# Where a head's row sums are closed: Q in slot 0, the fold on GpSimd, a first block written by ScalarE

## The reference

```python
x = layernorm(x + self_attention(x))                       # 32 heads of 16, causal, rotary
# cross-attention with ctx (4 x 1601 x 512): 32 query heads of 128, 8 key/value heads
q = (x @ Wq + bq).reshape(B, L, 8, 4, 128)
k, v = split(ctx @ Wkv + bkv)                              # 8 heads of 128 each
s = einsum('blkgd,bmkd->bkglm', q, k) / sqrt(128)
o = einsum('bkglm,bmkd->blkgd', softmax(s), v)
x = layernorm(x + o.reshape(B, L, 4096) @ Wo + bo)
x = layernorm(x + x @ base_W.T + top2_gated_lora(x))       # 28 experts of rank 8
```

## Time and profile before

| what | before |
|---|---|
| median of 3 runs | 3050.05 us (3045.78 to 3051.54) |
| profiled execution | 3042.88 us, span 3041.1 us |
| PE busy | 2831.5 us (93%) |
| DVE / ACT / POOL busy | 2171.2 / 1906.0 / 1570.0 us |
| chain that ended last | PE 78%, issue 7%, ACT 6%, POOL 3%, DVE 3%, DMA 2% |
| granted TensorE clock, mean | 0.985 |

### The profile page before, as it was taken

The page is one execution under the profiler, slowest core; times in us unless marked ns, Lnnn a source line. Parts: engine busy times, 40 slices in busy tenths (PEclk is TensorE's granted clock), DMA queues, the critical chain, the costliest instruction groups (busy, mean ns, idle before and its releaser), DMA issues.

```text
span 3041.1 us, 60253 instructions
## 1 busy us (share of the span) xinstructions
PE 2831.5 (93%) x20784; PEld 2619.2 (86%) x20784; DVE 2171.2 (71%) x4492; ACT 1906.0 (63%) x4264; POOL 1570.0 (52%) x1535
## 2 busy tenths in 40 slices
PE   7899999998899999999889999999978999999996
PEld 6789999997689999999668999999967899999985
DVE  5587777777558777777665877777756587878785
ACT  4476666665557666666565766666646576666663
POOL 4288787755125555555511645454542254555553
PEclk9999999998999999999899999999989999999998
DMA  5356564513311112121321112121222121212112
GB/s 186 134 190 208 165 215 162 178 50 115 103 42 56 70 64 77 63 77 63 121 89 43 65 62 77 64 77 56 80 111 89 36 84 42 97 43 91 50 53 97
DMA packets 97915, 285.08 MB, mean 94 GB/s; under 512 B 9936, under 2 KB 18256, under 8 KB 94416
## 3 DMA queue, kind: packets, MB, share of 16 engines
q1 hardware_dynamic: 97616, 281.24, 27.1%
HBM read 237.16 MB, written 44.04 MB: 92 GB/s over the span
## 4 chain that ended last, share of the span: by engine, by line
PE 78%; issue 7%; ACT 6%; POOL 3%; DVE 3%; DMA 2%; DVEq 0%; SPq 0%; ACTq 0%; POOLq 0%
PE bank L1012 41%; PE dn L1012 18%; PE sp L1012 14%; PE sp L1143 2%; ACT ph L702 2%; POOL kept_s L524 1%; ACT orw L713 1%; PE sp L1232 1%; PE sp L1083 1%; PE sp L1151 1%; ACT pn L629 1%; POOL lob L516 1%; DVE nmx L819 1%; POOL orw L536 0%; DMA wqk<-in_ws 0%
## 5 line engine op out<-in xcount | busy, mean ns | idle before, releaser
L524 POOL TENSOR_TENSOR kept_s<-kept_s,mrow 128x512 f32<-128x512 f32 (+1 forms) x896 | 1061.1, 1214 | 539.8 <-ACT mrow L692 539.8
L904 DVE TENSOR_TENSOR pl<-sp,ph 128x512 fp32r<-128x512 f32 (+1 forms) x896 | 577.0, 644 | 43.3 <-ACT sp L705 42.8
L702 ACT ACTIVATE ph<-kept_s 128x512 fp32r<-128x512 f32 (+1 forms) x896 | 534.8, 597 | 35.1 <-POOL kept_s L524 30.3
L1012 PE MATMUL dn<-ph,vh 128*128 128x256 f32 (+1 forms) x1664 | 492.5, 296 | 59.6 <-ACT orw L713 54.9
L705 ACT ACTIVATE sp<-kept_s 128x512 f32<-128x512 f32 (+1 forms) x896 | 506.3, 565 | 3.5 <-DVE sua L910 2.2
L910 DVE TENSOR_TENSOR sua<-sp,sua 128x512 f32<-128x512 f32 (+1 forms) x768 | 487.7, 635 | 0.0
L1012 PE MATMUL dn<-ph,vl 128*128 128x256 f32 (+1 forms) x1664 | 470.5, 283 | 0.0
L1012 PE MATMUL dn<-pl,vh 128*128 128x256 f32 (+1 forms) x1664 | 469.2, 282 | 0.0
L684 ACT ACTIVATE kept_s<-bank 128x512 f32<-128x512 f32 x384 | 229.0, 596 | 330.6 <-PE bank L1012 330.6
L1012 PEld LDWEIGHTS dn<-ph,vh 128*128 128x128 f32 (+1 forms) x1664 | 314.5, 189 | 95.2 <-ACT orw L713 86.6
L684 ACT ACTIVATE kept_s<-sp 128x512 f32<-128x512 f32 x384 | 229.6, 598 | 254.8 <-PE sp L1012 254.8
(11 more groups left out here) (147 smaller groups left out, 7009.0 us busy)
## 6 DMA issues: line engine op xcount, KB each, us to landing
wqx<-wq SPq DMA_DIRECT2D x128, 512.0 KB, 3.4
wox<-wo SPq DMA_DIRECT2D x64, 1024.0 KB, 4.9
wk<-wk SPq DMA_DIRECT2D x32, 512.0 KB, 4.5
wvx<-wv SPq DMA_DIRECT2D x16, 1024.0 KB, 5.8
raw<-in_ctx_t SPq DMA_DIRECT2D x48, 200.0 KB, 2.5
wqk<-in_ws SPq DMA_DIRECT2D x17, 513.0 KB, 3.9
raw<-in_wq_in SPq DMA_DIRECT2D x32, 256.0 KB, 3.8
wq<-hib SPq DMA_DIRECT2D x32, 256.0 KB, 2.0
```

The costliest lines, as they stand in the source:

```text
L524: nc.gpsimd.tensor_tensor(kept_s[:, n % 2, i:z, :], kept_s[:, n % 2, i:z, :], mrow[:, n % 2, :].unsqueeze(1).broadcast_to([P, z - i, S]), ...
L702: nc.scalar.activation(ph[:, k % PH, 0:cols], src, ACT.Exp, scale=XSCALE).then_inc(ph_ok, 1)
L904: nc.vector.tensor_tensor(pl[:, k % PH, 0:cols], src, ph[:, k % PH, 0:cols], ALU.subtract).then_inc(pl_ok, 1)
L1012: return nc.tensor.matmul(dst, lhs, rhs, start=first, stop=final)
```

## The change

Six things change together. The Q job of head h is run two slots earlier, in slot 0 instead of slot 2 (for head 1 at the first slot). There are three Q buffers instead of four. VectorE no longer copies the first block of exponentials to `sua`: ScalarE computes that block's exponential a third time, in place in `kept_s`, and VectorE's addition in the second slot takes the PSUM bank and `kept_s`. GpSimd adds the two halves of `sua` to `suc` (`fold_sums`, 128 x 256, new, in slot 5, ahead of its shift). TensorE's `sum_rows` is two matmuls on `suc` (4 records), in slot 6 and ahead of `weigh`; the reciprocals move to slot 6 on VectorE and their spread to slot 0 on TensorE, and `finish_head` one slot on. What guarded `sua` by `sx_mm` is now guarded by `sf_ok`, and `exponentials` waits for `pl_ok` and `su_ok` of two slots before. Context lines of the diff that say nothing are left out.

```diff
@@ -64,6 +64,7 @@
...
 PH = 4
+QH = 3
 NHD = 2 * G
@@ -72,7 +73,7 @@
...
 SCORE, SHIFT, EXP, LOW, VALUE = -13, -4, -3, -2, 0
-MAX_TURN, MAX_COL, MAX_ROW, SUM_COL, SUM_ROW, HEAD_SUM, HEAD_END = -6, -5, -4, 5, 6, 7, 8
+MAX_TURN, MAX_COL, MAX_ROW, SUM_FOLD, SUM_COL, SUM_ROW, HEAD_SUM, HEAD_END = -6, -5, -4, 5, 6, 7, 7, 9
 SLOTS = range(SCORE, NSL * (NHB - 1) + HEAD_END + 1)
@@ -105,7 +106,7 @@
...
     for h in range(1, NHB):
-        jobs[NSL * h + SCORE - 6].append(("Q",) + divmod(h, NHD))
+        jobs[max(NSL * h + SCORE - 8, SCORE)].append(("Q",) + divmod(h, NHD))
     for k in range(NHB // 2 - 1):
@@ -257,8 +258,8 @@
...
         kl = sb("kl", [P, LKP], F32R)
-        qh = sb("qh", [P, G, S], F32R)
-        ql = sb("ql", [P, G, S], F32R)
+        qh = sb("qh", [P, QH, S], F32R)
+        ql = sb("ql", [P, QH, S], F32R)
         vh = sb("vh", [P, KT, 2 * P], F32R)
@@ -272,6 +273,7 @@
...
         sua = sb("sua", [P, 2 * S])
+        suc = sb("suc", [P, S])
         mcol = sb("mcol", [P, TB])
@@ -303,6 +305,7 @@
...
         sb_ok, ph_ok, pr_ok, pl_ok, su_ok, sx_mm, rs_ok = (sem(n) for n in ("sb_ok", "ph_ok", "pr_ok", "pl_ok", "su_ok", "sx_mm", "rs_ok"))
+        sz_ok, sf_ok = (sem(n) for n in ("sz_ok", "sf_ok"))
         pv_mm, rd_mm, oc_ok, nm_ok, oh_ok, ot_ok = (sem(n) for n in ("pv_mm", "rd_mm", "oc_ok", "nm_ok", "oh_ok", "ot_ok"))
@@ -524,6 +527,13 @@
...
 
+            def fold_sums(b, h):
+
+                n = b * NHB + h
+                pool.wait_ge(su_ok, (n + 1) * (NSL - 1))
+                pool.wait_ge(sx_mm, n)
+                nc.gpsimd.tensor_tensor(suc[:, :], sua[:, 0:S], sua[:, S:2 * S], ALU.add).then_inc(sf_ok, 1)
+
             def finish_head(b, h):
@@ -552,6 +562,8 @@
...
                 for g in SLOTS:
+                    for h in head_of(g, SUM_FOLD):
+                        fold_sums(b, h)
                     for h, s in slot_of(g, SHIFT):
@@ -662,9 +674,9 @@
...
                         h = p * NHD + i
-                        if b * NHB + h >= G:
-                            act.wait_ge(sc_mm, (b * NHB + h - G + 1) * NSL)
-                        nc.scalar.activation(qh[:, h % G, :], src[:, 0:S], ACT.Identity,
+                        if b * NHB + h >= QH:
+                            act.wait_ge(sc_mm, (b * NHB + h - QH + 1) * NSL)
+                        nc.scalar.activation(qh[:, h % QH, :], src[:, 0:S], ACT.Identity,
                                              bias=cst[:, C_BQ + h:C_BQ + h + 1]).then_inc(*done)
@@ -701,8 +713,12 @@
...
                     if k >= 2:
-                        act.wait_ge(su_ok, k - 1)
+                        a, z = divmod(k - 2, NSL)
+                        act.wait_ge(pl_ok, k - 1)
+                        act.wait_ge(su_ok, a * (NSL - 1) + z)
                     nc.scalar.activation(pbank[k % 2][:, 0:cols], src, ACT.Exp, scale=XSCALE).then_inc(pr_ok, 1)
+                    if s == 0:
+                        nc.scalar.activation(src, src, ACT.Exp, scale=XSCALE).then_inc(sz_ok, 1)
 
@@ -861,8 +877,8 @@
...
                         h = p * NHD + i
-                        nc.vector.scalar_tensor_tensor(ql[:, h % G, :], src[:, 0:S], cst[:, C_BQ + h:C_BQ + h + 1],
-                                                       qh[:, h % G, :], ALU.add, ALU.subtract).then_inc(freed, 1)
+                        nc.vector.scalar_tensor_tensor(ql[:, h % QH, :], src[:, 0:S], cst[:, C_BQ + h:C_BQ + h + 1],
+                                                       qh[:, h % QH, :], ALU.add, ALU.subtract).then_inc(freed, 1)
                     else:
@@ -902,11 +918,13 @@
...
                     nc.vector.tensor_tensor(pl[:, k % PH, 0:cols], src, ph[:, k % PH, 0:cols], ALU.subtract).then_inc(pl_ok, 1)
-                    if s == 0:
-                        dve.wait_ge(sx_mm, n)
-                        nc.vector.tensor_copy(sua[:, 0:cols], src).then_inc(su_ok, 1)
-                    else:
-                        dve.wait_ge(su_ok, k)
+                    if s == 1:
+                        dve.wait_ge(sz_ok, n + 1)
+                        dve.wait_ge(sf_ok, n)
+                        nc.vector.tensor_tensor(sua[:, :], src, kept_s[:, n % 2, 0:2, :].rearrange("p t q -> p (t q)"),
+                                                ALU.add).then_inc(su_ok, 1)
+                    elif s:
+                        dve.wait_ge(su_ok, n * (NSL - 1) + s - 1)
                         nc.vector.tensor_tensor(sua[:, 0:cols], src, sua[:, 0:cols], ALU.add).then_inc(su_ok, 1)
@@ -1126,9 +1144,9 @@
...
                         dst, keys = sbank[k % 2][0:w, e * S:(e + 1) * S], slice(i * P, i * P + w)
-                        mm(dst, kh[:, keys], qh[:, h % G, :], True, False)
-                        mm(dst, kh[:, keys], ql[:, h % G, :], False, False)
-                        last = mm(dst, kl[:, keys], qh[:, h % G, :], False, True)
+                        mm(dst, kh[:, keys], qh[:, h % QH, :], True, False)
+                        mm(dst, kh[:, keys], ql[:, h % QH, :], False, False)
+                        last = mm(dst, kl[:, keys], qh[:, h % QH, :], False, True)
                     last.then_inc(sc_mm, 1)
@@ -1154,12 +1172,10 @@
...
                     n = b * NHB + h
-                    pe.wait_ge(su_ok, (n + 1) * NSL)
+                    pe.wait_ge(sf_ok, n + 1)
                     pe.wait_ge(mr_ok, n + (2 if h + 1 < NHB else 1))
                     for tb in range(TB):
-                        for e in range(2):
-                            last = mm(mbank[:, tb:tb + 1], sua[:, e * S + tb * P:e * S + (tb + 1) * P], cst[:, C_ONE:C_ONE + 1],
-                                      e == 0, e == 1)
+                        last = mm(mbank[:, tb:tb + 1], suc[:, tb * P:(tb + 1) * P], cst[:, C_ONE:C_ONE + 1], True, True)
                     last.then_inc(sx_mm, 1)
@@ -1246,12 +1262,12 @@
...
                         run_job(*j)
+                    for h in head_of(g, SUM_COL):
+                        sum_rows(h)
                     for h, s in slot_of(g, VALUE):
...
                         turn_maxima(h)
-                    for h in head_of(g, SUM_COL):
-                        sum_rows(h)
                 for j in LAST_JOBS:
```

## The result

The changed kernel takes 2958.93 us (median of 4 runs, 2956.39 to 2961.78) against 3048.85 for the one before: a ratio of 0.9702, 95% interval 0.9685 to 0.9718. That is 90 us, where 115 were forecast; the time lies in the range. The profiled execution's span went from 3041.1 to 2954.8 us, by 86.3.

A forecast was written before the change was run, and what follows sets the result against it. TensorE, busy 93% of the span, was taken as the bound. The terms -50 - 87 - 36 - 12 + 22 + 40 + 7 + 13 - 12 summed to -115 us, forecasting 2935 us, range 2880 to 3000.

The forecast's parts named there:

- (b): Slot 0: Q's matmuls cover ScalarE's copy, so TensorE's whole `orw` wait goes, -86.6 us.
- (a): TensorE's sums: four records instead of eight save 0.40 us for some 124 heads, -50 us.
- (c), (d): Reciprocals' wait in slot 6 goes, -36 us; two thirds of the `turn_maxima` wait in slot 1 goes, -12 us.
- (e): Slot 3: without Q in slot 2, TensorE waits for `mcol` in 12 heads a sequence, 0.45 us each, +22 us.
- (f): Slot 0: TensorE waits for reciprocals queued behind the next head's first addition on VectorE, +40 us (0 to +80).
- (g): The fold on GpSimd takes 0.74 us; 0.3 us in six heads where slots 4 and 5 are empty, +7 us.
- (h): First sequence: the fold lengthens GpSimd's queue, with weight splits ahead: 0.74 us for 18 heads, +13 us.
- (i): End of each sequence: GpSimd's last shift comes earlier, ahead of `finish_head`, -3 us in each of four, -12 us.
- only the records: Rival: waits of (b) and (c) reappear in slots 3 and 0; only -50 and -12 stay, 2988 us; chance 0.14.
- The new waits don't come: Rival: TensorE's jobs leave time, so (e) to (h) fall away wholly or half; priced at 2870 us; chance 0.13.
- The fold is late in every head: Rival: TensorE waits 0.6 us more for GpSimd's fold in each of 124 heads, 3010 us; chance 0.12.
- The slower case: Slot 0: (f)'s reciprocal wait in all 128 heads, with (e) in all heads, gives 3094 us; chance 0.06.

The follow-up runs named there:

- Q alone: The kernel before with only the Q job moved from slot 2 to slot 0: 2996.5 us, 0.9823.
- The run that takes this wait away: The changed kernel with `row_maxima` ahead of the difference and addition in VectorE's slot 2: 2925.7 us, 0.9596.
- the fold's run: The changed kernel with the fold on VectorE, right after the head's last addition, instead of GpSimd: 2945.5 us, 0.9664.
- the split moved: The changed kernel with the third weight piece of a head split in slot 5, behind the fold, instead of slot 4: 2970.0 us, 0.9744.
- the fastest kernel: The changed kernel with fold on VectorE, sums in slot 5 behind `weigh`, and row maxima first in VectorE's slot 2: 2903.5 us, 0.9522.

## Why the prediction was right, and where its size was off

The sign and the place of each new wait were as forecast; what each of the two halves is worth was not, see (b), nor was the clock. Of the missing 25 us the profile gives these, step by step.

- (a) Four records take 0.36 us (1823.36 to 1823.72) where eight took 0.81: 0.45 saved, 56 us for 124 heads, not 50.
- (b) 84 us of `orw` waits gone, 87 forecast. But it was credited to one edit where either one takes most of it: Q alone removed 76 us, and with the sums changed and Q in slot 2, 58 are gone already.
- (c), (d) The 36 us of slot 6 gone as forecast; `mxa` 16 and not 12.
- (e) +29 us, forecast 22. The term is under-sized: the 12 heads pay 0.56 us and more (slot 3 takes 2.19 instead of 1.63), and heads with a K job in slot 1 pay a further 0.1, as the slot times of 1.74 show. The run that takes this wait away gained 33.
- (f) +40.4 us, forecast 40. The walk was right to 0.1 us, and so were the heads in each of the last three sequences: five waits of 1.30 to 1.36 us, three of 0.77, four of 0.2, 9.8 us in all against 10.1. That the total agrees to 1% is in part luck: the first sequence has 4 us of these, and 1.7 a sequence come at its end, which (f) did not count.
- (g), (h) `suc` 22.9 us, 19.0 of it in the first sequence. The first sequence's cross-attention was 6 us longer than the others' before (620.0 against 613.8) and is 18 longer now (605.5 against 587.7 on average): 12, forecast 13. Part of the 12 is the clock's, since three of the six falls lie there; the fold's run above shows how these two go together.
- (i) The last scores to the last `weigh` went from 22.5 to 21.0 us a sequence: -6, not -12. The last shift indeed came first, but the reciprocal chain sets the rest. This was argued from the traces, not tried.

These make -56 - 84 - 36 - 16 + 29 + 40 + 23 - 6 = -106 us. The cross-attention became 93 shorter (2461.6 to 2368.7). The rest, 13, is the step that the prediction did not have: the granted clock. Every step priced a wait at its own length, and six waits were followed by TensorE at the lower clock, 27 us in all. At half speed these hold 13.6 us of lost work at most; at the 1.6 to 1.7 us read above from the three like sequences for a short one, four times, and twice that for each of the two long ones, it is 13. That the waits cause the falls is seen in their order only, and most waits of that length had none behind them; in the run with the `rs` waits longest in the first sequence (the split moved) there are 12 falls between the first and the last scores, and there are none in the runs with the sums in slot 5, with the sums behind `weigh` and with the row maxima first on top of them. But other waits will do: with the reciprocals first, four falls remain behind waits for `suc`, and with Q back in slot 2 and no `rs` wait there are three behind waits for `orw`. No run changed the clock alone.

The last 7 us between -93 and the span's -86.3 lie outside the cross-attention (579.5 to 586.1 us), which the change doesn't touch; the profiled executions vary by that much.

The rivals: "only the records" (62 us) is out, as the changed kernel gained 90 and the copy's and `mxa`'s waits are gone; what it said of new waits in slots 3 and 0 came true, at 29 and 40 us. "The new waits don't come" is out by the same two. "The fold is late in every head" is out: TensorE waited for it 13 times, 19.0 of the 22.9 us in the first sequence. The ratio of 1.8 that I had taken from the trace did not hold for the fold. Its 0.41 us was an operation with one operand in PSUM; the fold reads two from SBUF, and on VectorE it took 829 ns against GpSimd's 740. So VectorE's 13 us are not the operation's length. What the trace shows in their place is that the fold no longer stands behind GpSimd's splits in the first sequence: the `suc` waits went, other waits took most of their room, and two long falls went too. The Trainium skill (GPSIMD Engine Reference, "Engine selection") advises VectorE for an elementwise addition, as GpSimd is about 2 times slower. The run's time agrees with the advice, but the durations of this operation do not agree with the 2 times: here the measurement decides. The slower case, the `rs` wait in every head, came in 50 of 128, the heads named.

The forecast of which part brings the time was the weak point: I counted the Q move at 87 - 22 = 65 us and it is worth 5 in this kernel. It is worth 43 once the `rs` wait is removed.

## What to carry to other kernels

Two waits in the same slot of the bound engine hide each other: ask of each edit what it is worth with the others in place, and measure each alone and each left out. When a small operation is late, look at what stands ahead of it in its engine's program order before looking at the engine's load: changes of place (sums and reciprocals a slot earlier, the sums behind `weigh`, the row maxima ahead of work that had a slot in hand) and the fold on VectorE brought another 55 us, to 2903.5, with the same matrix work. Where a change adds waits of a microsecond and more to a busy TensorE, leave room in the range for the clock beside their length; and where two runs differ by some 10 us, compare the parts that the edit doesn't touch before giving it the whole. An operation's length on another engine is to be read from one with its operands in the same memories, beside the same neighbours.

## What the runs showed of the hardware

**VectorE and GpSimd on SBUF.** The fold on VectorE (two operands in SBUF) took 0.42 to 0.43 us in 8 heads of 128 and 0.48 to 1.53 in the other 120. In each of these 120 it ended some 0.28 us after the end of a GpSimd instruction, most of them shifts of 1.25 us, as if it could not begin its work before. GpSimd's shifts became longer as well, 1215 to 1237 ns on average, the longest 1323 and 1560. VectorE's operations with one operand in PSUM, among the same shifts, show nothing of it: 128x512 differences took 673 to 693 ns in that run and 675 to 693 in the kernel before. In the fastest kernel the fold takes 926 ns on average, and TensorE's waits for it are 9.3 us in all.

**TensorE's clock.** A matmul of 256 columns starts 0.117 us after the last at the full clock and 0.21 us at the lower one. Of the six falls in the changed kernel two came with the longest waits for `suc` (4.25 and 3.33 us), one behind one of 1.82, three behind waits for `rs` of 1.35 to 1.36 (by the weight loads; the one shown above is 1.35 so read). But 24 other waits of 1.30 to 1.82 us for `suc`, `rs` and `mcol`, up to each sequence's last `weigh`, had no fall behind them, the one of head 10 above too (one of 1.31, at the end of the first sequence, had a seventh behind it), and the kernel before stayed at the full clock behind six waits for `orw` of 1.48 to 2.02. With Q back in slot 2, three of four waits for `orw` of 2.10 had a fall behind them and the fourth had none. So the length of the one wait doesn't decide, and what does is open. The prediction had no term for it: it took the full clock that the cross-attention had before.

These are windows of the kernel before behind three of those six waits (1.91, 2.02 and 1.48 us), granted clock 1.00:

```profile
518.00:522.00 4.00, 3.17 (x27) 3.17 (x28) 3.48 (x7) 3.61 (x8) 3.92 (x5) 1.00 0.74 251
536.00:540.00 4.00, 3.66 (x31) 3.66 (x32) 3.69 (x8) 3.36 (x8) 3.92 (x5) 1.00 0.97 366
553.00:557.00 4.00, 3.72 (x31) 3.72 (x32) 3.47 (x8) 3.36 (x8) 3.92 (x5) 1.00 0.99 343
```
